# Layer changes cut into 512-column steps, four staging buffers, the last residual inside the loop, and the gated columns' low halves made on VectorE

## What is computed

```python
# once: adaLN modulation, causal attention, x1 = x + gate1 * attn(...)
# xk = layernorm(x1) * (1 + scale2) + shift2, second 64 channels shifted by one token
for layer in range(6):
    qkv = x @ Wqkv                       # 128 -> 3072
    q, k = l2norm, scale, rotary(q, k)   # tables of cos, sin times q_scale, k_scale
    x = x + local_attention(q, k, v) @ Wo
    xn = layernorm(x) * g + b
    a, gate = split(xn @ W1 + b1)        # 341 columns each
    x = x + (a * gelu(gate)) @ W2 + b2
out = x1 + gate2 * x                     # the last residual
```

## Time and profile before

| | us |
|---|---|
| median of 3 runs | 3763.39 |
| lowest and highest | 3753.32, 3766.66 |
| the profiled execution's own time | 3756.22 |
| its span, first to last instruction | 3754.2 |

### The profile page before, as it was taken

The page is one execution under the profiler, slowest core; times in us unless marked ns, Lnnn a source line. Parts: engine busy times, 40 slices in busy tenths (PEclk is TensorE's granted clock), DMA queues, the critical chain, the costliest instruction groups (busy, mean ns, idle before and its releaser), DMA issues.

```text
span 3754.2 us, 162428 instructions
## 1 busy us (share of the span) xinstructions
PE 3392.6 (90%) x72292; PEld 2052.2 (55%) x72292; DVE 2955.4 (79%) x3116; ACT 2601.3 (69%) x3315; POOL 3107.4 (83%) x2468
## 2 busy tenths in 40 slices
PE   7999999589998999989999889999899998989995
PEld 4666666355554555555555555555455555555553
DVE  7888887677887887878777778777788787887774
ACT  6777776467776666776677766776766777767773
POOL 3555556589998999989899988999899998989992
PEclk9999999799999999999999999999999999999997
DMA  1000000244545454545454544454444454545442
GB/s 62 5 5 8 5 5 24 75 112 114 122 107 118 95 117 108 117 109 116 93 127 108 117 100 106 114 122 105 113 102 110 116 116 106 119 95 116 104 108 80
DMA packets 162053, 347.53 MB, mean 93 GB/s; under 512 B 32588, under 2 KB 42064, under 8 KB 155088
## 3 DMA queue, kind: packets, MB, share of 16 engines
q1 hardware_dynamic: 161360, 337.15, 38.4%
HBM read 24.54 MB, written 4.19 MB: 8 GB/s over the span
## 4 chain that ended last, share of the span: by engine, by line
PE 50%; POOL 12%; DVE 7%; issue 6%; ACT 5%; SPq 1%; DMA 0%; DVEq 0%; POOLq 0%; ACTq 0%
PE psB L673 26%; PE psA L673 21%; POOL sq L1387 3%; PE psB L730 2%; DVE h L1289 2%; PE psA L730 1%; ACT sq L980 1%; POOL pb L1407 1%; POOL h L1382 1%; POOL h L1383 1%; POOL f_c L1412 1%; DVE ts L1281 1%; POOL n_a L1397 1%; POOL n_a L1394 1%; POOL n_b L1402 1%
## 5 line engine op out<-in xcount | busy, mean ns | idle before, releaser
L1362 POOL TENSOR_TENSOR pt<-wk,pt 128x256 f16<-128x256 f32 (+3 forms) x256 | 368.2, 1455 | 284.1 <-ACT pt L903 194.5
L1387 POOL TENSOR_TENSOR sq<-sq 128x512 f32<-128x512 f32 x384 | 487.3, 1281 | 82.7 <-ACT sq L980 82.4
L1382 POOL TENSOR_TENSOR h<-h,ts 128x512 f32<-128x512 f32 x384 | 503.1, 1310 | 35.3 <-DVE ts L1281 35.3
L1383 POOL TENSOR_TENSOR h<-h,ts 128x512 f32<-128x512 f32 x384 | 496.9, 1294 | 0.0
L1407 POOL TENSOR_TENSOR pb<-pb,rc 128x1024 f32<-128x1024 f32 x192 | 365.5, 1904 | 63.2 <-DVE rc L1302 60.5
L1300 DVE TENSOR_REDUCE sum<-pb 128x16 f32<-128x1024 f32 x192 | 232.9, 1213 | 108.5 <-ACT pb L1013 108.5
L1273 DVE TENSOR_TENSOR h<-psB,t_rot 128x1024 f32<-128x1024 f32 x192 | 233.6, 1217 | 77.1 <-ACT sq L980 72.6
L673 PE MATMUL psA<-kf,qf 64*32 64x64 f32 x18432 | 250.7, 227 | 29.3 <-issue 28.0
L980 ACT ACTIVATE sq<-psA 128x1024 f32<-128x1024 f32 x192 | 196.1, 1022 | 109.3 <-PE psA L673 109.2
L1273 DVE TENSOR_TENSOR h<-psA,t_rot 128x1024 f32<-128x1024 f32 x192 | 233.5, 1216 | 35.4 <-DMA kf<-h 13.9
L980 ACT ACTIVATE sq<-psB 128x1024 f32<-128x1024 f32 x192 | 196.2, 1022 | 88.2 <-PE psB L673 87.7
(11 more groups left out here) (364 smaller groups left out, 11040.7 us busy)
## 6 DMA issues: line engine op xcount, KB each, us to landing
qf<-h SPq DMA_DIRECT2D x768, 136.0 KB
kf<-h SPq DMA_DIRECT2D x768, 136.0 KB, 2.8
vev<-vo SPq DMA_DIRECT2D x192, 256.0 KB
vev<-vo SPq DMA_DIRECT2D x192, 224.0 KB
stage<-wqk SPq DMA_DIRECT2D x12, 512.0 KB, 5.3
stage<-wvl SPq DMA_DIRECT2D x12, 256.0 KB, 5.5
stage<-wof SPq DMA_DIRECT2D x6, 512.0 KB, 4.7
xb<-xt SPq DMA_DIRECT2D x8, 256.0 KB, 7.9
```

What stands on the lines that cost most here:

```text
L1362: e.tensor_tensor(pt[g][pr][:, :, 1, o:o + w], wk[(slot_of(s)[0] - 1) % SLOTS][:, :, 0:w], pt[g][pr][:, :, 0, o:o + w], ALU.subtract).then ...
L1382: e.tensor_tensor(halves_of(h, 0), halves_of(h, 0), t[1], ALU.subtract)
L1383: e.tensor_tensor(halves_of(h, 1), halves_of(h, 1), t[0], ALU.add).then_inc(ended["ad"])
L1387: e.tensor_tensor(sqb[c][:, 0, :], sqb[c][:, 0, :], sqb[c][:, 1, :], ALU.add).then_inc(ended["qa"])
```

## The change

`stage` becomes four buffers of 512 columns, filled in eight pieces for each layer (`piece_of`): pieces 0 to 2 and 3 to 5 are the two halves of the heads, 6 and 7 Wo. Pieces 0 to 3 are loaded together, 4 to 7 as buffers come free. `wh`, `wl`, `oh`, `ow` work on one piece of 512 columns each, `tb` on one of four tables (two instructions each), W1 and W2 become steps `wf` and `ws` of two parts each, and all of them are words of the strings, put at different places of two or three rounds. PE's waits name the piece they need and stand at a layer's first item alone.

The low halves `gl` go from POOL to DVE. The last residual becomes part of `fr` in the last layer: y is x1 from DRAM (loaded early to `kept`, the space of `t_tab` and `stage`), plus gate times `xb`, plus gate times `fo`, four instructions instead of two. Memory fills and two small scalings at the start of the layers go from DVE to POOL. All five strings are written anew in another order, and every PSUM user is now given a fixed pair (A to D), where `ss`, `op`, `la` and `fo` take one half of a pair.

```diff
-    "fm0 bm12 bm13 tc01+1 ts01+1 fm2 tc03+1 ol10 ts03+1 tc02+1 wl1 ts02+1 ol11 fm1 mx00+1 tc10+1 ts10+1 sm00+1 mx01+1 "
-    "rs bm00+1 bm01+1 sm01+1 bm02+1 bm03+1 ln+1 tc11+1 ol00+1 ts11+1 tc13+1 ts13+1 tc12+1 wl0+1 mx10+1 ts12+1 sm10+1 "
-    "ol01+1 tc00+2 mx11+1 ts00+2 fr ow bm10+1 bm11+1 sm11+1 "
+    "ts12+2 gl0+1 wl02+2 mx10+2 tc00+3 ts00+3 mx11+2 fr+1 sm10+2 bm10+2 bm11+2 fm1+2 sm11+2 ws0 fm0+2 wl01+3 wl11+2 "
+    "fm2+2 bm13+2 bm12+2 ol10+2 wl12+2 tc01+3 tc03+3 ts03+3 ts01+3 tc02+3 ow1+1 ol11+2 mx01+3 ts02+3 wl10+3 ow0+1 "
+    "wf0+1 mx00+3 sm01+3 tc10+3 sm00+3 wf1+1 ts10+3 rs+2 bm00+3 bm01+3 gl1+2 bm03+3 bm02+3 ln+3 tc11+3 ts11+3 gl2+2 "
+    "tc13+3 ol00+3 ts13+3 tc12+3 wl00+4 ws1 ol01+3 "
...
+        def weights_low(e, v, x, j):
+            e.wait_ge(*done("wh", v, x, j))
+            e.scalar_tensor_tensor(out=head_weights(1, x, j), in0=stage[(3 * x + j) % 4][:, :], scalar=WS,
+                                   in1=head_weights(0, x, j), op0=ALU.mult, op1=ALU.subtract).then_inc(ended["wl"])
...
                 elif kind == "tb":
-                        e.wait_ge(*all_done("ts", *((v - 1, x) for x in range(4))))
-                    for k in range(2):
-                        for h in range(2):
-                            for y in range(2):
+                    k, h = divmod(s[2], 2)
+                        e.wait_ge(*all_done("ts" if h else "tc", *((2 * v - 1 - x, k + 2 * i) for x in range(2) for i in range(2))))
+                    e.activation(t_rot[:, k, h, 0, :], t_tab[:, 2 * k + h, :], ACT.Copy, scale=t_scl[:, li, 2 * k:2 * k + 1])
...
+                elif kind == "gl":                       # now in local_vector, gone from local_gpsimd
+                    e.wait_ge(*done("gh", v, j))
+                    e.tensor_tensor(f_gl[j][0:n, :], f_g[j][0:n, :], f_gh[j][0:n, :], ALU.subtract).then_inc(ended["gl"])
...
+                    if li == L - 1:
+                        y = kept[b]
+                        e.wait_ge(s_x1d[b], 32)
+                        e.scalar_tensor_tensor(out=y[0:64, :], in0=xb[0:64, b, 0:S], scalar=t_mod[0:64, 5, b:b + 1],
+                                               in1=y[0:64, :], op0=ALU.mult, op1=ALU.add).then_inc(s_y)
...
+                        e.scalar_tensor_tensor(out=y[0:64, :], in0=o[0:64, 0:512], scalar=t_gz[0:64, b:b + 1], in1=y[0:64, :],
+                                               op0=ALU.mult, op1=ALU.add).then_inc(s_z)
```

More of the change, by code:

```diff
@@ L202, in ordinals, with plan_banks @@
     return count
-def plan_pairs(steps, rings):
-    at, had, place = {"A": 0, "B": 0}, {}, {}
+ONE_BANK = ("ss", "op", "la", "fo")
+def plan_banks(steps, homes):
+    user, place = [None] * 8, {}
     for s in steps:
[L209 to L214, removed]
+        if s in homes:
+            at = 2 * "ABCD".index(homes[s][0]) + (homes[s][1:] == "r")
+            own = range(at, at + (1 if s[0] in ONE_BANK else 2))
+            place[s] = (at, sorted({user[i] for i in own if user[i]}))
+            for i in own:
+                user[i] = s
     return place
@@ L318, in program @@
         t_gs = sb("t_gs", [128, L])
+        t_gz = sb("t_gz", [128, NB])
+        kept = [t_tab[:, b, :] for b in range(4)] + [t[:, :] for t in stage]
         x1d = nc.dram_tensor("x1_keep", [NB, 128, S], F32).ap()
@@ L338, in program @@
         s_wa = sems("s_wa", 3)
-        s_const, s_first, s_cin, s_x, s_wo, s_wm, s_w1, s_w2, s_tab, s_stage, s_x1r = (
-            sem("s_" + n) for n in ("const", "first", "cin", "x", "wo", "wm", "w1", "w2", "tab", "stage", "x1r"))
+        s_const, s_first, s_cin, s_x, s_wo, s_wm, s_w1, s_w2, s_tab = (
+            sem("s_" + n) for n in ("const", "first", "cin", "x", "wo", "wm", "w1", "w2", "tab"))
+        s_stage = sems("s_stage", 4)
         s_dm = sems("s_dm", 4)
@@ L344, in program @@
         s_out = sem("s_out")
-        s_masks, s_pads, s_chain, s_silu, s_mod, s_actc, s_z = (sem("s_" + n) for n in ("masks", "pads", "chain", "silu", "mod", "actc", "z"))
+        s_masks, s_pads, s_chain, s_silu, s_mod, s_actc, s_z, s_y = (sem("s_" + n) for n in ("masks", "pads", "chain", "silu", "mod", "actc", "z", "y"))
         s_lnq, s_lnl, s_lnr, s_lnn = (sems("s_" + n, 2) for n in ("lnq", "lnl", "lnr", "lnn"))
@@ L415, in psum @@
         def psum(s):
-            return pair[place[s][0]]
+            at = place[s][0]
+            return pair[at // 2][:, 512 * (at % 2):512 * (at % 2) + 512] if s[0] in ONE_BANK else pair[at // 2]
         def made(v, c):
@@ L462, in sync @@
                         e.wait_ge(*full(("c_op", b)))
-                        heads_of(e, 0, 0)
+                        for p in range(4):
+                            piece_of(e, 0, p)
                         e.dma_start(flat(t_tab), tab).then_inc(s_tab, 16)
@@ L500, in sync @@
                 li, u = divmod(v, 2 * NB)
+                if li == L - 1 and u < NB:
+                    if u < 4:
+                        e.wait_ge(*all_done("tb", *((NB * li, j) for j in range(4))))
+                    elif u < 6:
+                        e.wait_ge(*all_done("wl", (NB * li - 1, 1, 1), (NB * li - 1, 1, 2)))
+                    else:
+                        e.wait_ge(*done("ow", NB * li - 1, u - 6))
+                    e.wait_ge(s_x1d[u], 16)
+                    e.dma_start(kept[u], x1d[u]).then_inc(s_x1d[u], 16)
@@ L501, in sync @@
                 if u == 6 and li + 1 < L:
-                    e.wait_ge(ended["ow"], li + 1)
-                    heads_of(e, li + 1, 0)
+                    e.wait_ge(*all_done("wl", (NB * li - 1, 1, 1), (NB * li - 1, 1, 2)))
+                    e.wait_ge(*all_done("ow", (NB * li - 1, 0), (NB * li - 1, 1)))
+                    for p in range(4):
+                        piece_of(e, li + 1, p)
                 if u == 8 and li + 1 < L:
                     e.wait_ge(*done("lb", NB * li))
-                    e.wait_ge(s_w1s, li + 1)
@@ L507, in sync @@
-                    e.wait_ge(s_w2s, li + 1)
+                    e.wait_ge(*done("wf", NB * li - 1, 1))
+                    e.wait_ge(*done("ws", NB * li - 1, 1))
                     feed_of(e, li + 1)
-            e.wait_ge(*done("ss", 2 * NB * L - 1))
-            for b in range(NB):
-                e.dma_start(sqb[b // 2][:, b % 2, :], x1d[b]).then_inc(s_x1r, 16)
             for b in range(NB):
                 e.wait_ge(s_z, b + 1)
-                e.dma_start(out[b], sqb[b // 2][:, b % 2, :]).then_inc(s_out, 16)
+                e.wait_ge(*done("fr", NB * (L - 1) + b))
@@ L515, in sync, with piece_of @@
+                e.dma_start(out[b], kept[b]).then_inc(s_out, 16)
             e.wait_ge(s_out, 16 * NB)
-        def heads_of(e, li, half):
-            e.dma_start(stage[:, 0:1024], wqk[li, :, 1024 * half:1024 * half + 1024]).then_inc(s_stage, 16)
-            e.dma_start(stage[:, 1024:1536], wvl[li, :, 512 * half:512 * half + 512]).then_inc(s_stage, 16)
+        def piece_of(e, li, p):
+            to = stage[p % 4]
+            if p >= 6:
+                e.dma_start(to.rearrange("p (a c) -> p a c", a=4),
+                            wof[li, 512 * (p - 6):512 * (p - 5)].rearrange("(a p) c -> p a c", p=128)).then_inc(s_stage[p % 4], 16)
+            elif p % 3 == 2:
+                e.dma_start(to[:, :], wvl[li, :, 512 * (p // 3):512 * (p // 3) + 512]).then_inc(s_stage[p % 4], 16)
+            else:
+                at = 1024 * (p // 3) + 512 * (p % 3)
+                e.dma_start(to[:, :], wqk[li, :, at:at + 512]).then_inc(s_stage[p % 4], 16)
@@ L675, in take @@
             def take(s):
-                slot, before = place[s]
-                if before:
+                for before in place[s][1]:
                     k, at = before[0], before[1:]
@@ L687, in take @@
                         e.wait_ge(*done(LAST[k], *at))
-                return pair[slot]
+                return psum(s)
             for s in tensor_walk:
```

233 lines of the change are left out of this document (116 added, 117 removed), and 17 rows, old and new, of tables (SCALAR, TENSOR).

## The result

The changed kernel takes 3815.59 us (median of 4 runs, 3796.12 to 3824.27) against 3764.34 us for the kernel before (4 runs beside it): a ratio of 1.0135, 95% interval 1.0089 to 1.0181. It is 51 us slower, a small difference whose interval leaves out 1, where 164 us less were forecast. The profiled execution took 3821.09 us, its span is 3819.3 us.

What follows compares the result with a forecast made beforehand. POOL and PE were both taken as near the bound in stretches without a layer change, with chain waits at changes. Gains 94 + 47 + 12 + 5 = 158 us off 3754.2, with 2 around it, gave 3598, taken as 3600; range 3525 to 3700.

Steps and rivals of the forecast that it cites:

- Layer changes: At the five layer changes: small steps remove three quarters of the 125 us excess, 94 us off, between 0 and 125.
- Rival 4: At layer changes: excess is the pipeline draining, whatever the step size; only end and start gain, 3739 us; chance 0.07.
- Steady gain: In items generally: 1.0 us off each of 47 items, 47 us; bounds 2.5 off and 3 on.
- `gl`: Three instructions per item moved from POOL to DVE at 1.4 us each: POOL falls to 54.6 us, DVE rises to 51.7.
- Rival 3: In each item: `gl` makes DVE the bound and delays PE, items grow by 3.0 us, 3840 us; chance 0.08.
- Rival 2: In items: the shared path of DVE and POOL eats the steady gain, half the change excess goes, 3677 us; chance 0.20.
- The last residual: At the kernel's end: moving 16 instructions off the path behind the last `fr` gains 12 us.
- the cover: In the last eight items: DVE's free time of 7.8 us hides the residual's extra instructions; without it, up to 27 us.
- Start and SP: Start: fills to POOL, W1/W2 halves later, gain 5 us (0 to 5.5); SP's queue costs nothing, 10 us if wrong.

Runs made afterwards that it cites:

- x7: x3 with the last residual put back behind the loop, as in the kernel before: 3686.6 us, ratio 0.9773.
- x3: Kernel before with small layer-change steps, ring of four weight buffers and last residual in the loop; old orders, PSUM plan, `gl` on POOL: 3700.27 us, ratio 0.9807.
- x3d: x3 with `gl` on VectorE: 3718.11 us, ratio 0.9851.
- x2: The kernel before with `gl` alone moved to VectorE, in the old orders: 3771.16 us, ratio 0.9994.
- x1: The changed kernel with `gl` moved back from VectorE to GpSimd (POOL), in the new orders: 4095.48 us, ratio 1.0855.
- z1: The changed kernel with three runs of matmuls that wait for nothing added behind its last item, on TensorE alone: 3943.84 us in one run.
- x4: The changed kernel with 11 of the 57 words of TensorE's order moved by one or two places: 4170.15 us, ratio 1.1064.
- x8: x3 with three of TensorE's steps moved by one to three places to thin out dense stretches: 3744.12 us, ratio 0.9932.

## Why the prediction was wrong, step by step

By the ratios, the change is made of four parts: small steps and ring -0.0227 (x7), 85 us off; the last residual in the loop +13 us (x3 to x7); `gl` on VectorE +17 us (x3 to x3d); the new orders and PSUM plan +107 us. They add up to the measured 51 by their making, each ratio less the one before, so the sum is no check of them. The second is not clear of the noise.

*Layer changes.* The mechanism was right and its size nearly: 94 forecast, and x7's five stretches with a change take 1238.4 us where they took 1315.0, 77 less with the old orders (the 85 above are of the whole kernel). In x7 a stretch with a change takes 247.7 us on average and the others 239.4: an excess of 8 us instead of 25, two thirds gone where I took three quarters. Rival 4 falls. The tables' share can be seen in PE's wait for the copy of v, before and changed (x7 has none):

```profile
PE psB L673 <- ACT vo L1006: 22.9, 5, 4.9
```

```profile
PE psB L693 <- ACT vo L1036: 0.6, 2, 0.4
```

These are the waits that rows 3 show at one change; the 5.85 us read there are idle time of the weight loads, and the matmuls waited 4.9 us at most. How much the tables, the blocks of halves and PE's waits by piece each gave was not run apart.

*Steady gain.* This is the step that failed: "I take 1.0 us off each of 47 items", with bounds of 2.5 off and 3 on. It came out at 4.3 us **on** in the items without a change, outside both bounds, and with a cause that was in no rival: TensorE stood for instructions 113 us longer. Nor was the 1.0 us there in the old orders: x7's items without a change take 59.9 us each, 0.4 more than before. I looked for what an item could lose in the four busy shares and in the waits for semaphores. The 83 us of "issue" in the kernel before stood in its waits already, and I gave them no row. I had written that the rows can't tell the sign of the new orders; then a term of -47 us with half the chance behind it was not to be taken. Without standing time the new orders would have been worth something: x3d to the changed kernel is +107 us in time and +130 us in standing time (38 to 168), which leaves some 23 us of gain; with all pauses (79 to 191) the two differ by 5 us the other way. That is an inference, not a run, and it goes from 23 us down to nothing with the way of counting.

*`gl`.* The durations (ns, least, median, most) were near the assumed 1.4 us, a little shorter:

```profile
L1367 DVE TENSOR_TENSOR f_gl<-f_g,f_gh x144: 675/1193/1854, 863.0 to 3810.7; 128x512 f16<-128x512 f32 x96, 85x512 f16<-85x512 f32 x48
```

POOL gave up 7.5 us in four items for the forecast 8. Rival 3 needed DVE as the bound, and DVE is at 83%; PE waits for `f_gl` 12.8 us in all. Rival 2, the path that both engines share, can't be large: POOL's two additions take 1.34 and 1.30 us on average where they took 1.31 and 1.29, and the whole move costs 17 us in x3d and nothing in x2. What it costs in the new orders no run shows, since x1 failed at that.

*The last residual.* The gain at the end came, 43.2 us from the last `rs` to the end of the span before and 31.3 now, 12 as forecast. What failed is the cover: "cost up to 27 if that cover were gone" is what happened, 21 us in one stretch of x3 and some 9 in the changed kernel.

*Start and SP.* The first `rs` is 5.3 us earlier (795.28 for 800.55), but one item later nothing is left of it (859.34 for 859.29). No wait for SP's loads stands among PE's longer ones.

## What to carry over

When an order is rewritten, count instructions along each engine as well as microseconds: where a long row of TensorE's instructions would issue faster than 256 in about 3.5 us, the row can cost the difference, however well the semaphores are met. It is a rate and not a rule for each 256: if the engine has just been slower, one packet lies ready, and in the kernel before 256 instructions went out in 1.72 us without a pause (from 2502.41 us). Read the "issue" line of the waits first; if it is not near zero, a busy share below the bound is not free room. And try each part of a change in the old order before giving all of it a new one: here 85 us of gain lay under 137 us of loss.

## What the runs showed of the hardware

TensorE's instruction stream is a bandwidth of its own: packets of 256 instructions, never closer than 3.23 us in the 15 traces here (x3; 3.27 in the kernel before), and one each 3.47 to 4.02 us in a dense run where nothing else works (z1). Dense steps use them in 1.80 to 2.04 us (z1). The Trainium skill (Advanced Engine Details and Errata, ISA Cache) describes lines of 16 KB, 256 instructions, and says "Only 2 cache lines!"; the trace agrees with the 256 (574 packets for 147071 instructions) and with so short a reserve (the pauses end 1.2 to 1.7 us behind a landing). Runtime: NRT & Kernel Launch (section Instruction fetch mechanics) holds the crossing to be "mostly hidden", since instructions go out more slowly than they are filled in; the 1.43 to 1.98 us between the blocks of z1 say otherwise, and the measurement decides.

A step order that fits is worth more than I thought: moving 11 steps by one or two places cost 350 us (x4), three steps 47 us (x8). What part of the granted clock's fall, 1.00 to 0.97 in stretches without a change, is a cause and what follows from the pauses was not separated.
